# One opening order changed in an attention and FFN kernel: gate-weight absolutes on DVE, Wv and half of Wo squared on ACT

## What is computed

```python
x = x + _L0_xattn_ref(_layernorm(x), ctx, Wq, Wk, Wv, Wo, gq, gk)   # 16 batches, 128 tokens, 16 heads of 128
x = x + _L0_ffn_ref(_layernorm(x), w_gate, w_up, w_down, ln_weight)

# attention
q = rmsnorm((h @ Wq).reshape(B, Sq, H, D), gq)
k = rmsnorm((c @ Wk).reshape(B, Skv, H, D), gk)
attn = softmax(einsum('bqhd,bkhd->bhqk', q, k) * scale)
out = einsum('bhqk,bkhd->bqhd', attn, v).reshape(B, Sq, H * D) @ Wo

# ffn: weights are rounded to -1, 0, 1 times their mean absolute value
def weight_quant(w):
    s = 1.0 / clip(mean(abs(w)), EPS, None)
    return clip(round(w * s), -1.0, 1.0) / s
h = silu(bit_linear(x, w_gate)) * bit_linear(x, w_up)
```

## Time and profile before

| | |
|---|---|
| median of three runs | 471.62 us (471.61 to 473.48) |
| the profiled execution | 473.02 us, of which the span is 470.9 us |
| DVE busy | 430.5 us, 91% |
| ACT busy | 428.6 us, 91% |
| PE busy | 413.0 us, 88% |
| POOL busy | 391.1 us, 83% |
| granted TensorE clock, mean | 0.995 |

### The profile page before, as it was taken

One profiled execution on the slowest core, in us unless ns is written; L12 is line 12 of the kernel. 1 busy time (PEld: TensorE's weight loads), 2 busy tenths in 40 slices (PEclk: granted clock), 3 DMA queues, 4 the chain that ended last, 5 costly groups with the idle time before them and its releaser, 6 DMA issues.

```text
span 470.9 us, 14733 instructions
## 1 busy us (share of the span) xinstructions
PE 413.0 (88%) x4554; PEld 319.4 (68%) x4554; DVE 430.5 (91%) x1249; ACT 428.6 (91%) x1454; POOL 391.1 (83%) x362
## 2 busy tenths in 40 slices
PE   0399867889999999999999999999999679789886
PEld 0388654777787777777777787777777455556555
DVE  3789899899999999999999999999898868999995
ACT  3488899999999999999999999999999679999982
POOL 2034958799999999999999999999999966888882
PEclk9999999999999999999999999999999999999998
DMA  8941824265354354354354354354466541001001
GB/s 292 431 170 24 307 51 91 59 121 137 89 118 106 89 114 109 89 117 106 89 114 109 89 120 103 90 116 108 92 102 105 133 68 24 13 22 36 22 33 57
DMA packets 140238, 50.18 MB, mean 107 GB/s; under 512 B 135856, under 2 KB 137904, under 8 KB 139312
## 3 DMA queue, kind: packets, MB, share of 16 engines
q1 hardware_dynamic: 139920, 48.78, 41.9%
q10 hardware_dynamic: 288, 1.05, 0.6%
HBM read 14.16 MB, written 2.10 MB: 35 GB/s over the span
## 4 chain that ended last, share of the span: by engine, by line
ACT 28%; POOL 27%; issue 20%; DVE 14%; PE 6%; DMA 3%; POOLq 1%; SPq 0%; DVEq 0%; ACTq 0%
ACT work L706 10%; POOL rkq L553 8%; POOL work L543 6%; POOL phl L565 6%; ACT kjunk L744 5%; ACT qshl L728 4%; POOL qshl L530 3%; ACT qhl L638 3%; DVE ham L1241 3%; ACT work L730 2%; ACT ohl L755 2%; DMA stage<-in_wqP 2%; POOL stage L607 1%; POOL hrr L613 1%; DMA kT<-khl 1%
## 5 line engine op out<-in xcount | busy, mean ns | idle before, releaser
L706 ACT ACTIVATE work<-SO,nbias,rkq 128x128 f32<-128x128 f32 x256 | 115.9, 483 | 2.2 <-DVE nbias L1080 2.1
L553 POOL TENSOR_TENSOR rkq<-kqe,negh 128x8 f32<-128x8 f32 x65 | 109.7, 1688 | 4.2 <-DVE kqe L1067 3.7
L381 PE MATMUL KQ<-hT,wqs 128*128 (+1 forms) x1536 | 99.3, 221 | 8.7 <-DVE wqs L929 6.7
L381 PEld LDWEIGHTS KQ<-hT,wqs 128*128 128x128 f16 x1536 | 91.9, 99 | 14.4 <-issue 11.7
L381 PE MATMUL EB<-As,ohl 128*128 128x256 f16 x768 | 94.3, 273 | 0.4 <-issue 0.4
L530 POOL TENSOR_TENSOR qshl<-work,qshl 128x512 f16<-128x512 f32 x64 | 74.6, 1165 | 23.5 <-ACT work L730 23.5
L381 PEld LDWEIGHTS EB<-As,ohl 128*128 128x128 f16 x768 | 75.1, 98 | 22.7 <-issue 0.8
L565 POOL TENSOR_TENSOR phl<-work,phl 128x512 f16<-128x512 f32 x64 | 74.1, 1158 | 12.2 <-DVE phl L1151 10.4
L543 POOL TENSOR_TENSOR work<-work,rinv 128x512 f32<-128x512 f32 x64 | 66.7, 1041 | 4.6 <-DVE rinv L1025 4.6
L381 PEld LDWEIGHTS SO<-kT,qhl 128*128 128x128 f16 x768 | 44.5, 98 | 28.8 <-DMA kT<-khl 18.6
L381 PE MATMUL SO<-kT,qhl 128*128 128x128 f16 x768 | 53.5, 219 | 9.0 <-DMA kT<-khl 5.0
(11 more groups left out here) (164 smaller groups left out, 937.6 us busy)
## 6 DMA issues: line engine op xcount, KB each, us to landing
xs<-in_xP SPq DMA_DIRECT2D x4, 512.0 KB, 21.0
stage<-in_wqP SPq DMA_DIRECT2D x4, 512.0 KB, 10.6
wvo<-in_woP SPq DMA_DIRECT2D x1, 2048.0 KB, 17.9
out<-wqs SPq DMA_DIRECT2D x16, 128.0 KB, 1.7
raw<-in_ctxT ACTq DMA_DIRECT2D x1, 1024.0 KB, 6.5
wvo<-in_wvP SPq DMA_DIRECT2D x1, 1024.0 KB, 13.5
raw<-in_ctxP SPq DMA_DIRECT2D x1, 1024.0 KB, 19.9
kT<-khl SPq DMA_TRANSPOSE x64, 2.8
```

What stands on the lines that cost most here:

```text
L381: last = matmul(out, lhsT=left(i), rhs=right(j), start=start and n == 0, stop=stop and n == 2)
L553: pool.tensor_tensor(rkq[:, g % 4, :], kqe[:, g % 2, :], negh[:, 0:2 * HG], ALU.pow).then_inc(root_ok, 1)
L706: ins = act.activation(pe[:, s, c], SB[:, c], ACT.Exp, scale=rkq[:, (g - AT_X + 1) % 4, HG + h:HG + h + 1], bias=nbias[:, s, h:h + 1], acc ...
```

## The change

It touches the opening alone. The loop, the drain and the FFN keep their instructions and their order.

1. The absolutes of the gate weights are summed by a DVE reduction in step 4. ACT keeps those of up (step 6) and down (step 7). The three weight loads signal three semaphores in place of one.
2. The squares of Wv (step 0) and of the second half of Wo (step 1) are summed on ACT, each by one pass over 2048 columns, into the buffer of A. The first half of Wo stays with Gram products, 16 in step 0 in place of 48 in steps 0 to 2. The three sums go to PE, which adds them up.
3. The scale of A is made in step 1 in place of step 2, and the products of A start in step 2 in place of step 3.
4. Nearly all lists of calls of `fill` and `early` are put in another order, and the tables move splits, statistics, layer norms and context pieces between steps.

The diff, cut; of the reordered bodies those of ACT's `fill` and DVE's `early` stand here:

```diff
-A_AT = {3: (0, 4), 4: (4, 6), 5: (6, 8)}
-TOT_AT = 2
-SQ_AT = {0: (0, 2), 1: (2, 4), 2: (4, 6)}
-STAT_AT = {1: (1, 2), 2: (2, 3), 3: (3, 4)}
-ROOT_AT = {1: (1, 2), 3: (2, 4)}
-APPLY_AT = {0: (2, 4), 2: (4, 8), 4: (8, 12), 6: (12, 16)}
-C_AT = {2: (0, 1), 3: (1, 4)}
-ABS_AT = {5: 0, 6: 1, 7: 2}
+A_AT = {2: (0, 2), 3: (2, 4), 4: (4, 6), 5: (6, 8)}
+TOT_AT = 1
+SQ_AT = {0: (0, 1), 1: (2, 3)}
+GRAM_AT = 0
+STAT_AT = {0: (1, 2), 1: (2, 4)}
+ROOT_AT = {1: (1, 2), 2: (2, 4)}
+APPLY_AT = {0: (2, 4), 1: (4, 8), 3: (8, 12), 4: (12, 14), 5: (14, 16)}
+C_AT = {1: (0, 1), 2: (1, 2), 3: (2, 3), 4: (3, 4)}
+ABS_AT = {6: 1, 7: 2}
+ABS_DVE = 4
...
-        HI_AT = {'start': (0, 3), 1: (3, 9), 2: (9, 11), 4: (11, 12)}
-        LO_AT = {'start': (0, 1, 2), 0: (3, 4, 5, 6, 7), 1: (8,), 5: (9, 10), 6: (11,)}
+        HI_AT = {'start': (0, 3), 0: (3, 9), 1: (9, 10), 2: (10, 12)}
+        LO_AT = {'start': (0, 1, 2), 0: (3, 4, 5, 6), 1: (7,), 2: (8,), 5: (9,), 6: (10, 11)}
...
+            def A_squares(at):
+
+                for i in range(*SQ_AT.get(at, (0, 0))):
+                    act.wait_ge(wvo_in[0 if i else 1], 16)
+                    src = wo_f[:, H // 2 * i - H // 2:H // 2 * i, :] if i else wvT_f
+                    act.activation(As[:, i % 2, H // 2 * (i // 2):H // 2 * (i // 2) + H // 2, :].rearrange("p h n -> p (h n)"),
+                                   src.rearrange("p h c -> p (h c)"), ACT.Square,
+                                   accum_out=ssA[:, i:i + 1]).then_inc(sumA_ok, 1)
...
             def fill(b, g):
+                A_squares_at(b, g)
+                ln_highs(b, g)
+                splits_at(b, g)
+                q_pieces(b, g)
+                c_highs(b, g)
                 ffn_absolutes(b, g)
-                splits_at(b, g)
-                c_highs(b, g)
-                q_pieces(b, g)
-                ln_highs(b, g)
                 k_squares(b, g)
                 A_outs(b, g)
...
+            def ffn_absolute(b, g):
+                if now(b, g) == ABS_DVE:
+                    dve.wait_ge(ffn_in[0], 16)
+                    dve.tensor_reduce(absum[:, 0:1], stage[:, 0:2048], axis=AX_X, op=ALU.add,
+                                      apply_absolute_value=True).then_inc(wabs_ok, 1)
...
+            def early(b, g):
+                ffn_absolute(b, g)
+                x1_stats(b, g)
+                splits_at(b, g)
                 ln_lows(b, g)
+                p_sums(b, g)
+                psum_consts(b, g)
+                A_scale(b, g)
                 k_high(b, g)
                 k_low(b, g)
...
+            def gram(b, g):
+                if now(b, g) == GRAM_AT:
+                    te.wait_ge(wvo_in[0], 16)
+                    for h in range(H // 2):
+                        for k in range(KT):
+                            w = wo_f[:, h, k * P:(k + 1) * P]
+                            ins = te.matmul(SB[:, 0:P], lhsT=w, rhs=w, start=h + k == 0, stop=h + k == H // 2)
+                    ins.then_inc(gram_ps, 1)
```

More of the change, by code:

```diff
@@ L184, in build_program @@
         g_in = sem("g_in")
-        ffn_in = sem("ffn_in")
+        ffn_in = [sem(f"ffn_in{i}") for i in range(3)]
+        wabs_ok = sem("wabs_ok")
         consts = sem("consts")
@@ L686, in ln_highs, with A_squares_at @@
                     ln_high(now(b, g) - 1)
+            def A_squares_at(b, g):
+                A_squares(now(b, g))
             def c_highs(b, g):
@@ L767, in early @@
                 ln_highs(b, g)
-                splits_at(b, g)
-                exponentials(b, g)
-                q_pieces(b, g)
-                A_outs(b, g)
-                ffn_absolutes(b, g)
-                k_squares(b, g)
-                c_highs(b, g)
-                o_high(b, g)
+                exponentials(b, g)
+                A_squares_at(b, g)
+                q_pieces(b, g)
+                c_highs(b, g)
+                ffn_absolutes(b, g)
+                o_high(b, g)
+                k_squares(b, g)
+                A_outs(b, g)
+                splits_at(b, g)
             def step(b, g):
@@ L1311, in wvo_product @@
                 ins.then_inc(A_ps, 1)
-            def grams(at):
-                for i in range(*SQ_AT.get(at, (0, 0))):
-                    te.wait_ge(wvo_in[0 if i >= 2 else 1], 16)
-                    m = slice(0, CD) if i < 2 else slice(P * (i % 2), P * (i % 2) + P)
-                    src, lo = (wvT_f, 8 * i) if i < 2 else (wo_f, 8 * (i // 2 - 1))
-                    o = SB[:, 0:P] if i < 2 else SB[:, P:2 * P]
-                    for h in range(lo, lo + 8):
-                        ins = te.matmul(o, lhsT=src[:, h, m], rhs=src[:, h, m],
-                                        start=h == 0 and i in (0, 2), stop=h == H - 1 and i in (1, 5))
-                    ins.then_inc(gram_ps, 1)
             te.wait_ge(consts, 9)
@@ L1413, in scores @@
                     s, r = (g - AT_S) % 2, (g - AT_S) % 4
-                    if now(b, g) == AT_S:
-                        te.wait_ge(sumA_ok, 1)
                     need_dma(te, kT_in[s], b, g, AT_S)
@@ L1445, in ln_transposed @@
                 ln_transposes(now(b, g) if now(b, g) >= 0 else None)
-            def grams_at(b, g):
-                grams(now(b, g))
+            def gram(b, g):
[6 more added lines that the diff above has]
+                    ins.then_inc(gram_ps, 1)
             def A_total(b, g):
                 if now(b, g) == TOT_AT:
-                    te.wait_ge(sumA_ok, 1)
+                    te.wait_ge(sumA_ok, 3)
                     te.wait_ge(qse_ok, TOT_AT)
-                    te.matmul(MB[:, 4:6], lhsT=ones_f[:, :], rhs=ssA[:, :], start=True, stop=True).then_inc(totA_ps, 1)
+                    for c, i in ((4, 0), (5, 1), (5, 2)):
+                        ins = te.matmul(MB[:, c:c + 1], lhsT=ones_f[:, :], rhs=ssA[:, i:i + 1],
+                                        start=i < 2, stop=i != 1)
+                    ins.then_inc(totA_ps, 1)
                     for s in wvo_in:
```

106 lines of the change are left out of this document (49 added, 57 removed).

## The result

| | median | runs |
|---|---|---|
| before | 472.31 us | 10, 471.35 to 473.48 |
| after | 473.89 us | 10, 472.77 to 475.44 |
| ratio | 1.0037 | 95% interval 1.0024 to 1.0049 |

The change makes the kernel 1.6 us slower by the medians, 1.1 to 2.3 by the interval. That is less than 0.5%, and it is outside the noise. The forecast, 473.1 us, was made on a median of 471.62 us and so means 1.5 us more than before. The size was right. In every ratio of this document the executions that ran slow are left out: one of c2 (691.76 us), the profiled one of e4 (478.93 us) and one of the kernel before that was timed beside e1 to e4 (1060.05 us).

The account below looks back on a forecast made before the run. DVE was taken to bound the opening, which sets when the loop begins: 0.9 us from DVE's stretch plus 0.6 us for PE's slow clock, 1.5 us, took the median from 471.62 to 473.1 us; range 470.0 to 475.6.

Parts of the forecast that it names:

- DVE is the bound up to the exponentials of step 6, not ACT: In the opening, DVE sets when the exponentials of step 6 start, and ACT is idle ahead of those of steps 5 and 6.
- The rival in which ACT is the bound: In the opening, DVE is ready whenever ACT is; exponentials of step 6 start 2.5 us sooner, 469.1 us; chance 0.17.
- Start at 21.56: DVE's stretch from the second maxima to the `biases` of step 6 starts at 21.56 in place of 23.35.
- Length 48.56, without the clock: DVE's stretch from the second maxima to the `biases` of step 6 takes 48.56 us in place of 45.23.
- the collision that I kept for the layer norms: On DVE, 0.4 us kept because the two layer norms in step 5 may meet POOL's operation of line 530.
- Exponentials of step 6 at 70.2, 0.9 later: On ACT, the exponentials of step 6 start at 70.2 in place of 69.31, 0.9 us later.
- The gate's load has landed: The gate weights land near 53, ahead of DVE's reduction near 55, a cover of 2 us.
- Gram products and squares on ACT are free: In the opening, two Gram blocks leaving PE (3.73 us each) gain nothing, and ACT's two added passes of squares cost nothing.
- The clock falls in step 1, one A product runs at half clock, 0.6 us: PE stands nearly idle over 3 us in step 1, its clock falls, one A product runs slowly: 0.9 - 0.3 = 0.6 us.
- the rival of the cancelling pieces: The clock falls harmlessly or returns ahead of the A products, and DVE saves small waits: 471.9 us; chance 0.20.
- POOL passes the start on one for one: At 4.85 us a step on POOL, any shift of the loop's start goes to the end one for one.
- The sum: For the opening, 0.9 us of later exponentials plus 0.6 us of slow clock, 1.5 us, giving a median of 473.1 us.

Follow-up runs that it names:

- c2: e2 with 120 filling instructions in PE's program, 80 at the head and 40 behind the first transposes, two gaps where PE waits; ratio 0.9982 to the kernel before.
- e4: e3 with six more unused fp32 products on PE in step 7, behind the scores; ratio 1.0038 to the kernel before.
- e1: The changed kernel with the DVE reduction over the gate weights done twice in step 4; ratio 1.0089 to the kernel before.
- e2: The changed kernel with the absolutes of the gate weights back on ACT in step 5; ratio 1.0011 to the kernel before.
- e5: The changed kernel with both passes of squares on ACT (Wv, half of Wo) done twice; ratio 1.0029 to the kernel before.
- e6: The changed kernel with five unused fp32 products on PE ahead of the scores in each of steps 64 and 65; ratio 1.0055 to the kernel before.
- c1: e2 with 120 filling instructions at the head of PE's program; ratio 1.0041 to the kernel before.
- p1: The changed kernel with 120 instructions that do nothing at the head of PE's program; ratio 1.0068 to the kernel before.
- b1: The kernel before with only the gate absolutes moved from ACT to a DVE reduction in step 4; ratio 1.0045 to the kernel before.
- p2: The kernel before with 136 instructions that do nothing at the head of PE's program; ratio 1.0137 to the kernel before.
- e3: The changed kernel with ten more unused fp32 products on PE in step 1, behind the transposes; ratio 1.0045 to the kernel before.

## Why the prediction was right, and where it was not

- **DVE is the bound up to the exponentials of step 6, not ACT.** Right: ACT waits 2.15 and 1.29 us for DVE, e1 costs the whole reduction, e2 gives it back until ACT takes over. The rival in which ACT is the bound falls.
- **Start at 21.56.** Measured 21.33.
- **Length 48.56, without the clock.** Measured 48.52, and that agreement is luck, since it is not of the same parts: it has the 0.60 us behind the slow clock, which I had counted apart, and 0.85 us of `nbias` held up. In e5, which has neither, it was 47.37. Of the 1.2 us between, 0.4 are the collision that I kept for the layer norms, 0.36 the slow `rstd` of before that I left in the base; the rest I have not taken apart.
- **Exponentials of step 6 at 70.2, 0.9 later.** Measured 70.04, 0.7 later; 69.13 and 69.34 in e5 and e6, whose DVE work is the change's.
- **The gate's load has landed, Gram products and squares on ACT are free.** Right: no idle time ahead of 55.37, and e5.
- **The clock falls in step 1, one A product runs at half clock, 0.6 us.** Right in the trace: fall at 37.3, one product of 1.71 us, a wait of 0.60 us. The fall came in all eight traces that fill nothing there, but its cost differs: no wait in e1, e2, e5 and e6, where the clock was back ahead of the A products as in the rival of the cancelling pieces, 0.19 in c1, 0.29 in p1, 0.60 in the change, 0.72 in c2. So 0.6 us was too much on the average, and neither filling bought time. The working also passed over one row of before: its queries of step 0 took 2.72 us at 20.38, behind 6.75 us without work for PE, though the granted clock reads 1.00 there. The second fall at 85.1 was not foreseen; DVE waited 0.22 us for it and POOL waited for ACT, so I see no cost there.
- **POOL passes the start on one for one.** Right in most of the steps, and wrong as a whole. From step 8 to step 59 the change takes 258.20 us and before 257.74, c2 257.03 and e2 258.73. Wrong was thus the sentence that what the change can move is *therefore* when the loop begins. It also moved where PE's code lies, and through that the length of the loop.
- **The sum.** 0.9 + 0.6 us was forecast for the opening. By the ratios, the reduction on DVE costs 1.2 us (e2 to the change; 2.1 in b1), the place of the code 1.4 to 1.9 us (c2 against e2, p2, p1; each with an uncertainty of about 1 us), and the rest of the reordering gains some 0.9 us (c2). That is 1.2 + 1.5 - 0.9 = 1.8 us, and the ratio of 1.0037 is 1.7. With c2 against e2 for the middle term such a sum comes out right by its making, so it is a way to divide the loss and no proof; p1, p2 and the traces, which give 1 to 2 us, are the independent evidence for that term. The forecast had the right total from an opening that alone, by this sum, costs about 0.3 us, because it counted from one profiled execution in which DVE had lost over a microsecond by chance, and because it lacked the place of the code. That the two errors made up for each other is luck.

What stays open: that the load of q8 delays the transposes rests on their standing together in the traces and on moving the code there and back; how the load does it, no run shows. The times of the p runs need a subtraction of 3.4 and 5.0 us to say it, and only one execution of each kernel is profiled. Why e3, whose traced loop is short, was slow over its runs is not explained. Nor have I shown what makes the clock come back in time in some executions.

## What to carry to other kernels

Work that is hidden on one engine is not free for the kernel if it is removed or added: the length of an unrolled head moves the code of everything behind it, and an instruction load can land on a transfer that nothing covers, here at one step inside a loop whose own code was not touched. Measure the length of such a loop inside the trace before calling it unchanged. Before costing an edit in a stage of 50 us to a tenth, compare two profiled executions of the same code, since one of them can hold a microsecond of chance. And test edits that depend on each other together: here the early maxima alone lost 1.8 us, and in the whole reordering they were part of a gain of some 0.9.
